# A mixture of experts computed only for the chosen tokens, with rows sorted by expert through DRAM, in place of every expert for every token

## The reference

```python
def _moe_forward(hidden_states, gate_w, gate_bias, eg_w, eu_w, ed_w, sg_w, su_w, sd_w):
    x = hidden_states.reshape(-1, H)
    shared = jax.nn.silu(x @ sg_w.T) * (x @ su_w.T) @ sd_w.T
    scores = jax.nn.sigmoid(x @ gate_w.T) + gate_bias
    group_scores = scores.reshape(T, G, E // G).max(axis=-1)
    _, sel_groups = lax.top_k(group_scores, TG)
    ...
    topk_w, topk_i = lax.top_k(masked_scores, K)
    topk_w = topk_w / (topk_w.sum(axis=-1, keepdims=True) + 1e-08)
    comb = jnp.zeros((T, E), x.dtype).at[jnp.arange(T)[:, None], topk_i].add(topk_w)
    h = silu(einsum('th,eih->eti', x, eg_w)) * einsum('th,eih->eti', x, eu_w)
    routed = jnp.einsum('eti,ehi,te->th', h, ed_w, comb)
    return (shared + routed).reshape(B, S, H)
```

## Time and profile before

| | us |
| --- | --- |
| median of three runs (1149.51, 1150.63, 1157.2) | 1150.63 |
| span of the profiled execution | 1143.3 |
| start and full attention (0 to 421.5) | 421.5 |
| experts M1 (421.5 to 713) | 291.5 |
| banded attention (713 to 861) | 148.0 |
| experts M2 (861 to 1143.3) | 282.3 |
| PE busy, share of the span | 1044.1, 91% |
| DVE busy, share of the span | 925.3, 81% |

### The profile page before, as it was taken

How to read it: one execution, slowest core, us unless ns; L and a number is a source line. 1 busy time by engine, 2 the same in 40 slices (tenths; PEclk the granted TensorE clock), 3 DMA queues, 4 the chain that set the end, 5 groups by cost and what they waited for, 6 DMA issues and landing times. The chain is left out here.

```text
span 1143.3 us, 18866 instructions
## 1 busy us (share of the span) xinstructions
PE 1044.1 (91%) x6314; PEld 427.5 (37%) x6314; DVE 925.3 (81%) x2139; ACT 709.0 (62%) x1089; POOL 461.7 (40%) x434
## 2 busy tenths in 40 slices
PE   5769999999999979999999998888888999999998
PEld 4212222222222325444444443334444444444443
DVE  8688999999998467889788776877876779877775
ACT  2537778777787765666666664355465566666664
POOL 4116336532100105565564554100113556556554
PEclk9758999999999989999999999679999999999999
DMA  6901302311200126566764873142206667687662
GB/s 207 253 2 28 81 9 72 80 53 28 54 2 1 43 59 170 163 170 174 196 181 140 218 193 81 34 110 59 72 4 172 157 152 188 171 208 193 182 189 57
DMA packets 72185, 131.63 MB, mean 115 GB/s; under 512 B 12680, under 2 KB 47624, under 8 KB 72088
## 3 DMA queue, kind: packets, MB, share of 16 engines
q1 hardware_dynamic: 68704, 120.92, 40.5%
q10 hardware_dynamic: 3384, 9.51, 3.1%
HBM read 115.08 MB, written 14.91 MB: 114 GB/s over the span
## 5 line engine op out<-in xcount | busy, mean ns | idle before, releaser
L421 ACT ACTIVATE Aatt_prob<-Aatt_st 128x1024 f32<-128x1024 f32 x256 | 247.7, 1022 | 66.1 <-PE Aatt_st L315 65.1
L487 DVE TENSOR_REDUCE Aatt_mx<-Aatt_sc 128x1 f32<-128x512 f32 x439 | 273.3, 683 | 10.0 <-PE Aatt_sc L302 9.5
L1993 POOL TENSOR_TENSOR M1ex_low<-M1ex_hid,M1ex_high 128x512 f16<-128x512 f32 x132 | 152.8, 1157 | 136.2 <-ACT M1ex_high L1892 70.1
L1993 POOL TENSOR_TENSOR M2ex_low<-M2ex_hid,M2ex_high 128x512 f16<-128x512 f32 x132 | 152.7, 1157 | 130.8 <-PE M2ex_acc L1848 73.3
L302 PE MATMUL Aatt_sc<-ks,qs 48*128 48x512 bf16 x496 | 152.5, 408 | 29.5 <-DVE Aatt_mx L487 11.8
L1886 ACT ACTIVATE M2ex_sil<-M2ex_ring,unscale 128x512 f32<-128x512 f32 x132 | 90.7, 687 | 95.3 <-PE M2ex_ring L1831 95.1
L1886 ACT ACTIVATE M1ex_sil<-M1ex_ring,unscale 128x512 f32<-128x512 f32 x132 | 90.7, 687 | 89.4 <-PE M1ex_ring L1831 88.9
L327 PE MATMUL Aatt_pv<-Aatt_prob,vg 128*32 128x512 f32 x1024 | 137.9, 611 | 0.6 <-ACT Aatt_prob L421 0.6
L1930 DVE SCALAR_TENSOR_TENSOR M2ex_ring<-M2ex_ring,unscale,M2ex_sil 128x512 f32<-128x512 f32 x132 | 100.0, 757 | 42.0 <-ACT M2ex_sil L1886 38.9
L1930 DVE SCALAR_TENSOR_TENSOR M1ex_ring<-M1ex_ring,unscale,M1ex_sil 128x512 f32<-128x512 f32 x132 | 99.9, 757 | 36.2 <-ACT M1ex_sil L1886 32.9
L302 PEld LDWEIGHTS Aatt_sc<-ks,qs 48*128 48x128 bf16 x496 | 35.9, 94 | 201.1 <-DVE Aatt_mx L487 167.7
(11 more groups left out here) (437 smaller groups left out, 1959.5 us busy)
## 6 DMA issues: line engine op xcount, KB each, us to landing
M1ex_cb<-comb SPq DMA_DIRECT2D x130, 256.0 KB, 4.1
M2ex_cb<-comb SPq DMA_DIRECT2D x130, 256.0 KB, 4.2
M_wt<-wsplit SPq DMA_DIRECT2D x132, 192.0 KB, 4.0
wsplit<-split_cut SPq DMA_DIRECT2D x9, 704.0 KB, 4.5
qs<-stack SPq DMA_DIRECT2D x32, 96.0 KB
ks<-stack SPq DMA_DIRECT2D x30, 96.0 KB
split_raw<-in_wg_dram ACTq DMA_DIRECT2D x3, 704.0 KB, 8.5
split_raw<-in_wu_dram ACTq DMA_DIRECT2D x3, 704.0 KB, 12.0
```

What stands on the lines that cost most here:

```text
L421: act.activation(prob[e % 4][:, :, :].rearrange("p a c -> p (a c)"), st[pr][:, :, :].rearrange("p a c -> p (a c)"), ACT.Exp, scale=SCALE). ...
L487: ins = dve.tensor_reduce(mx[k][:, m, h:h + 1], scores, AX.X, ALU.max)
L1993: pool.tensor_tensor(low[q % 3][:, :], hid[q % 3][:, :], high[q % 3][:, :], ALU.subtract).then_inc(low_ready, 1)
```

## The change

In both layers of experts, each token's normalised row (high and low f16 part beside each other, 512 bytes) is now sent to the experts that it chose, and only those are computed.

- **Dispatch.** After the routing, new code (`dispatch_tensor`, `dispatch_vector`) counts the tokens of each expert, gives each expert as many blocks of 128 rows as it needs, and works out for each of a token's six choices the row in which it stands (`index`), and for each block the offset of its expert's weights (`expert`). A batch has a fixed number of 112 blocks, enough for any routing; blocks that are not needed are computed too.
- **Scatter.** POOL issues 48 indirect DMAs per batch (8 tiles of 128 tokens times 6 choices); each writes 128 rows to `slots_in` in DRAM.
- **Blocks.** Four blocks make a quad, 28 quads per batch, N = 56. SP loads a quad (512 rows, 256 KB) with a DMA that transposes it into one of three buffers, PE multiplies with the rows as the stationary side and with weights at an offset read from a register, and SP stores the quad's result rows (256 KB) to `slots_out`. Of a quad, `gate_up` has 12 matmuls of 128 columns and waits for its load and for `gate_times_up` of the quad two before; `turn` has four transposes, `down` eight matmuls. DVE copies the result out of PSUM (`evict`, 128x512) before it is stored. All routed weights lie in SBUF.
- **Gather.** POOL issues 48 indirect DMAs per batch that fetch each token's six result rows, and DVE adds them up with their weights (`combine`).
- **Order.** The output projection, normalisation, routing and dispatch of batch 1 and the shared expert now stand ahead of the loop over quads, and the normalisation and projection of batch 0 behind it.
- **Zero fill.** Since some rows of `slots_in` are never written, ACT issues two DMAs at the start of `attend_full` that fill both (14336 rows of 512 bytes each) with zeros.
- **Stores of split weights.** The nine pieces go to three tables instead of `wsplit`: six pieces in runs of 256 bytes, three in four DMAs each with runs of 512 bytes.
- **Removed.** `comb`, its turning, copies, store and loads; the weight loads per pair; POOL's low parts of the experts.

```diff
@@ attend_full
         def _(act):
             act.sem_inc(exp_done, FREE)
+            for rows in env.slots_in:
+                act.dma_start(rows.rearrange("(p a) c -> p a c", p=P),
+                              env.zero[:, :].rearrange("p (a c) -> p a c", a=1).to_broadcast([P, BLOCKS, 2 * C])).then_inc(env.zeroed, 16)
...
-            rest_of(route_vector(dve, env, q1))
-            for c in range(2):
-                dve.wait_ge(q1.comb_turned, c + 1)
-                dve.tensor_copy(q1.combT[:, c * CH:(c + 1) * CH], bank[c][0:ROWS, :]).then_inc(q1.comb_copied, 1)
+            rest_of(route_vector(dve, env, n1, q1, send))
+            rest_of(dispatch_vector(dve, env, q1, send, bank))
...
+def dispatch_vector(dve, env, q, send, bank):
...
+    dve.wait_ge(send.counted, 1)
+    done(dve.tensor_scalar(send.count[:, :], bank[1][:, 0:E], float(P - 1), None, ALU.add))
...
+    done(dve.tensor_tensor_scan(send.ends[:, :], env.ones_row[:, :], send.blocks[:, :], 0.0, ALU.mult, ALU.add))
...
+    dve.scalar_tensor_tensor(send.place[:, :, :], bank[0][:, :].rearrange("p (t e) -> p t e", t=TB), 1.0,
+                             q.of_experts.keep[:, :, :], ALU.add, ALU.mult).then_inc(send.place_ready, 1)
...
+    for t in range(TB):
+        dve.max(send.top[:, t, :], send.place[:, t, :]).then_inc(send.step, 1)
...
+    dve.tensor_scalar(send.index[:, :, :], send.top[:, :, :], 1.0, None, ALU.subtract).then_inc(send.index_ready, 1)
...
+def scatter_rows(pool, env, send, b):
...
+    pool.wait_ge(env.zeroed, 16 * B)
+    if b:
+        pool.wait_ge(send.index_ready, 1)
+        pool.wait_ge(send.low_ready, 2)
+    for t in range(TB):
+        for k in range(SLOTS):
+            pool.indirect_dma_start(env.slots_in[b], bass.IndirectOffsetOnAxis(
+                ap=send.index[:, t, k:k + 1].bitcast(U32), axis=0), send.row[:, t, :], None).then_inc(env.scattered[b], 16)
+            yield
...
@@ experts, SP
+            def load_quad(i):
+                b, g = i // QUADS, i % QUADS
+                if g == 0:
+                    sp.wait_ge(env.scattered[b], ALL_SENT)
+                if i >= X_RING:
+                    sp.wait_ge(gu_done, i - X_RING + 1)
+                sp.dma_start_transpose(rows_in[i % X_RING][:, :, :],
+                                       env.slots_in[b][g * CH:(g + 1) * CH, :]).then_inc(rows_loaded[i % X_RING], 16)
...
+            for i in range(N + 5):
+                if i < N:
+                    load_quad(i)
+                if i >= 5:
+                    store_quad(i - 5)
@@ experts, PE
+            rest_of(out_tensor(pe, env, o, bank, 1))
+            rest_of(norm_of_batch_tensor(pe, env, n1, bank))
+            rest_of(route_tensor(pe, env, n1, q1, bank))
+            rest_of(dispatch_tensor(pe, env, q1, sends[1], bank))
...
+            for i in range(N + 3):
+                if i < N:
+                    gate_up(i)
+                if 2 <= i < N + 2:
+                    turn(i - 2)
+                if i >= 3:
+                    down(i - 3)
@@ experts, DVE
+            for i in range(N + 4):
+                if i < N:
+                    gate_times_up(i)
+                if 1 <= i < N + 1:
+                    low_part(i - 1)
+                if i >= 4:
+                    evict(i - 4)
...
+                if i >= QUADS + 9 and (i - QUADS) % 3 == 0 and (i - QUADS - 9) // 3 < TB:
+                    combine((i - QUADS - 9) // 3)
@@ experts, POOL
+            rows = scatter_rows(pool, env, sends[0], 0)
+            for _ in range(16):
+                next(rows)
+            rest_of(norm_of_batch_gpsimd(pool, env, n1))
+            for _ in range(12):
+                next(rows)
+            rest_of(route_gpsimd(pool, env, n1, q1, sends[1], 1))
+            rest_of(rows)
+            rest_of(scatter_rows(pool, env, sends[1], 1))
+            for j in range(2 * TB):
+                gather(j)
```

More of the change, by code:

```diff
@@ L1564, in route_vector @@
     of_groups, of_experts = q.of_groups, q.of_experts
-    yield
-    yield
+    for c in range(2):
+        tiles = slice(4 * c, 4 * c + 4)
+        dve.wait_ge(n.xn_ready, 4 * c + 4)
+        dve.tensor_copy(send.row[:, tiles, 0:C], n.xn[:, tiles, :]).then_inc(send.high_ready, 1)
+        yield
     yield
@@ L1817, in _, with weights_of @@
         def _(pe):
[L1818 to L1821 removed]
+            registers = [[pe.alloc_register(f"{tag}_expert{i}_{j}") for j in range(4 * GROUP)] for i in range(2)]
+            of_block = {}
+            def weights_of(i):
+                b, g = i // QUADS, i % QUADS
+                handles = registers[i // GROUP % 2]
+                pe.load(handles, sends[b].expert[0:1, 4 * g:4 * g + 4 * GROUP])
+                for j, h in enumerate(handles):
+                    of_block[4 * i + j] = pe.snap(h, min_val=0, max_val=(E - 1) * 2 * P)
@@ new lines, in gate_up @@
+            def gate_up(i):
+                b, g = i // QUADS, i % QUADS
+                if i == QUADS:
+                    pe.wait_ge(sends[1].expert_ready, 1)
+                if g % GROUP == 0:
+                    weights_of(i)
+                pe.wait_ge(rows_loaded[i % X_RING], 16 * (i // X_RING + 1))
+                if i >= 2:
+                    pe.wait_ge(hid_ready, i - 1)
+                x = rows_in[i % X_RING]
+                for j in range(4):
+                    w = first[:, bass.ds(of_block[4 * i + j], 2 * P)].rearrange("p (g h c) -> p h g c", g=2, h=2)
+                    to = gu[i % 2][:, j * P:(j + 1) * P].rearrange("p (g c) -> p g c", g=2)
+                    rows = slice(j * P, (j + 1) * P)
+                    pe.matmul(to, x[:, 0, rows], w[:, 0, :, :], start=True, stop=False)
+                    pe.matmul(to, x[:, 0, rows], w[:, 1, :, :], start=False, stop=False)
+                    mm = pe.matmul(to, x[:, 1, rows], w[:, 0, :, :], start=False, stop=True)
+                mm.then_inc(gu_done, 1)
@@ L1866, in _ @@
-            beside, behind = before(), after()
-            for q in range(QN):
-                gate_up(q)
-                if q < HB:
-                    next(beside, None)
-                if q in (UPDATE, UPDATE + 1):
-                    back(0, q - UPDATE)
-                if q >= AFTER:
-                    next(behind, None)
-                if q >= LAG:
-                    down(q - LAG)
-            for q in range(QN - LAG, QN):
-                down(q)
-            for c in range(2):
-                back(1, c)
+                if c:
+                    pe.wait_ge(s_hid, c)
@@ L1900, in before @@
-            def before():
-                yield from out_scalar(act, env, o, bank, 1)
-                yield from norm_of_batch_scalar(act, env, n1, bank)
-                yield from route_scalar(act, env, n1, q1, bank, 1)
-            def after():
-                if not last:
-                    yield from norm_of_batch_scalar(act, env, n2, bank)
-                    yield from qkv_scalar(act, env, v2, bank, 0)
-            beside, behind = before(), after()
-            for q in range(QN):
-                silu(q)
-                if q:
-                    high_part(q - 1)
-                if q in (HB + LAG - 1, HB + LAG):
-                    add_up(0, q - HB - LAG + 1)
-                if q < HB:
-                    next(beside, None)
-                if q >= AFTER:
-                    next(behind, None)
@@ new lines, in _ @@
+            rest_of(out_scalar(act, env, o, bank, 1))
+            rest_of(norm_of_batch_scalar(act, env, n1, bank))
+            rest_of(route_scalar(act, env, n1, q1, bank, 1))
+            for c in range(NC):
+                shared(c)
+            for i in range(N + 2):
+                if i < N:
+                    silu(i)
+                if 1 <= i < N + 1:
+                    high_part(i - 1)
+                if i >= 2:
+                    copy_turned(i - 2)
+            if not last:
+                rest_of(norm_of_batch_scalar(act, env, n2, bank))
+                rest_of(qkv_scalar(act, env, v2, bank, 0))
@@ L1955, in after @@
-            def after():
-                if not last:
-                    dve.wait_ge(x_ready, 2)
-                    yield from norm_of_batch_vector(dve, env, n2, 0)
-                    yield from qkv_vector(dve, env, v2, bank, 0)
-            dve.tensor_copy(cb[0][:, :], env.unscale[:, 3:4].to_broadcast([P, S])).then_inc(cb_filled, 1)
-            dve.wait_ge(cb_filled, 1)
-            beside, behind = before(), after()
-            for q in range(QN):
-                times_up(q)
-                times_weight(q)
-                if q < HB:
-                    next(beside, None)
-                if q in (UPDATE, UPDATE + 1):
-                    update(0, q - UPDATE)
-                if q >= AFTER:
-                    next(behind, None)
@@ new lines, in _ @@
+            after = iter(())
+            if not last:
+                dve.wait_ge(combined, TB)
+                after = norm_of_batch_vector(dve, env, n2, 0)
+                for _ in range(6):
```

(8 more changed lines are left out.)

591 lines of the change are left out of this document (361 added, 230 removed).

## The result

The changed kernel takes 1367.47 us (median of four runs, 1354.11 to 1374.09) against 1150.07: a ratio of 1.188, 95% interval 1.180 to 1.196. It is slower by 217 us; 1487 was forecast. Its profiled execution has a span of 1367.0 us, 223.7 more than the span before.

| stage | before | after | difference | forecast |
| --- | --- | --- | --- | --- |
| start and full attention, to 421.87 / 459.40 | 421.9 | 459.4 | +37.5 | +59 |
| experts M1 | 288.7 | 375.6 | +87.0 | +133 |
| banded attention | 150.5 | 162.4 | +11.9 | +4 |
| experts M2, to the end | 282.3 | 369.6 | +87.3 | +140 |

A forecast was written before the change was run, and what follows sets the result against it. PE's matmuls bound M1 and M2; a ring of waits through SP's order would replace them. Span 1143.3 + 55 (zero fill) + 8 (dispatch) + 133 (M1) + 140 (M2) = 1479.3, plus 7.3: 1487 us; 8-in-10 range 1310 to 1710.

The forecast's parts named there:

- The loop: 56 quads in each of M1 and M2: 4.9 us per quad (3.8 to 6.4), 274 us per stage.
- The ring: Loop over quads: each load stands behind an earlier quad's store in SP's order; two quads take 9.8 us.
- L: Landing time of a quad's transposing load in the loop: 4.6 us, bounds 2.4 and 7.6.
- The four handovers: Waits between engines within two quads of the loop: 1.1 us together, an estimate.
- Ahead of the loop: Start of each experts stage: PE ready after 70.5 us, POOL's path ends at 73; loop starts at 74.
- c: What one indirect DMA costs POOL in scatters and gathers: 1.2 us, from 0.21 or 0.37 up to 2.86.
- Behind the loop: After the last quad: 8 us to finish and store, then gathers; 62 and 4 more in M2, 65 in M1.
- The zero fill: Start of full attention: two DMAs hold ACT's queue for 58 us, +55 (bounds 0 and 60).
- Dispatch: In both attentions it takes the place of turning and storing `comb`: +4 us each, +8.
- POOL as the pace: Rival, chance 0.15: indirect DMAs cost POOL 2 us or 2.86 us each; total about 1610 or 1810 us.
- The dearer load: Rival, chance 0.15: transposing load goes in eight pieces, landing 3.6 us later, 6.7 us per quad, total 1690.
- The fast rival: Rival, chance 0.10: engines pace the loop, 56 quads in 148 us, zero fill holds nobody; 1112 us, 3% faster.

The follow-up runs named there:

- the later store: Changed kernel with SP storing each quad's result one step later, behind i - 6 instead of i - 5: 1276.16 us, 1.112 of the kernel before.
- 72 blocks: 72 blocks per batch in place of 112, against the kernel with result stores one step later, zero fill on SP and scatters first: 1151.12 us, 0.999 of before.
- cutting its waits there: Against the 72-block kernel of 1151.12 us: POOL's five products for batch 1 made by DVE, six empty steps between batches on every engine: 1127.77 us, 0.982 of before.
- the opened ring: Changed kernel with result stores one step later: 1276.16 us with the transposing load, 1257.78 us with a plain load in its place.

## Why the prediction was right, and where it was off

**What bounds the kernel** was read rightly: the matmuls went (PE 1044 to 866 us busy) and the time rose, since what took their place is latency.

**The loop** was the largest error: 274 us forecast, 213.5 and 212.0 measured. That alone is 122 us too much, where the whole sum (1479.3 for the span) lay 112 too high; the other errors, on both sides, about cancel. The ring was the right mechanism, as the later store shows. Its terms were mis-sized: two quads take 7.6 us, not 9.8. The landing L was 3.6 to 3.7 at the median, not 4.6, some 1 us of the 2.2: I took it from plain loads of the same size, but a plain load in this very place lands after 3.3. L lay inside its bounds of 2.4 to 7.6. The four handovers, 1.1 us without a row, take some 0.3 together in the chain, 0.8 less, and the store's issue 0.36, not 0.5. Each is small, but the ring turns 56 times in the two loops.

The 0.11 us of a matmul of 128 columns was a wrong reading of the earlier trace rows: those four are of f32, at the upper clock. By the row of 512 columns in f16, 0.22, it is 0.055. That `gate_up` still took 1.3 to 1.5 us in the turns of the chain, near the 1.6 forecast, is luck: the clock was at its lower level for much of the loop.

The Trainium skill, "VectorE: DVE Perf Modes", section "The three transpose paths", gives 1309 ns for a 128x128 transpose by DMA, by which I estimated 10.5 us for a quad's eight. The trace does not agree with that use of it: 3.6 to 3.7 us at the median, so the eight do not follow each other.

**Ahead of the loop**, 74 was right within 2 us, for partly another reason. I let POOL wait for `inv` of batch 1 at 41 us; in the trace it never waited, because 28 scatters and four products kept it busy until 43 us. What decides is simply 48 x 1.26 and 7 us of products. c = 1.2 was near, 1.26, but by luck: its row is of an elementwise operation, and an indirect DMA's price stood in no row.

**Behind the loop** I put 8 for the drain and the last store; it was 13.6. Of the six stores that follow the last load, the last one was issued 10.5 us behind the last `gate_up`, since its quad still had to be turned, go down and be evicted. The gathers were 48 x 1.26 + 3, as forecast. In M1 I had the gathers wait for the projection (the ring of three buffers); they did not: POOL issued them from 762 to 825 without such a wait, and the 86 us are drain, gathers and the barrier.

**The zero fill** held ACT, +37.5 and not +55: the step that failed is that the issues last as long as both transfers. They lasted 39.1 us, about as long as the first transfer (41.9), while the second DMA landed 73.4 us after its issue. The Trainium skill, "Perfetto Trace Analysis", section "DMA Instruction — HWDGE (DVE, Sync)", lets the sequencer go on when all descriptors are generated; the trace agrees, with ACT free at 73 and the data there at 108.

**Dispatch** cost nothing in the full attention where +4 was forecast. In the banded attention the stage is 11.9 us longer. Its granted clock by stretch, the changed kernel and then the kernel before (columns as in the earlier trace rows), at the same distance from the stage's start:

```profile
923.00:931.00 8.00, 8.00 (x51) 4.42 (x50) 4.53 (x24) 1.90 (x6) 0.00 (x0) 0.50 0.00 0
963.00:971.00 8.00, 8.00 (x56) 5.15 (x52) 4.25 (x24) 3.56 (x10) 0.00 (x0) 0.50 0.00 1
```

```profile
798.50:806.50 8.00, 7.04 (x83) 4.61 (x83) 6.68 (x38) 3.59 (x10) 0.91 (x4) 1.00 0.01 3
838.50:846.50 8.00, 6.72 (x93) 2.71 (x88) 7.66 (x40) 4.70 (x13) 3.26 (x6) 1.00 0.03 6
```

The clock fell to its lower level (1.2 GHz) in two stretches where the kernel before had the upper one (2.4 GHz). Of the eleven traces of the changed kernel and its variants, all with the same code in this stage, eight have 161 to 163 us here and three 153 to 156, and the one of these that I read by stretch (154.0, with the later store) keeps the upper level from 80 us into the stage on. So some 8 of the 11.9 us come with the lower clock, in the same code. The 3 to 4 that are left look like the 4 forecast for dispatch, but they aren't: from the end of the last `keep` of the routing to the first PE instruction of M2, where dispatch stands in place of `comb`, it is 8.2 us in the kernel before, 9.5 in the changed kernel and 8.0 with the later store. They are lost ahead of that, and where, like what lowered the clock, stays open.

**The rivals.** POOL as the pace did not decide here, but it comes close with 72 blocks: 192 x 1.26 = 242 of the 280 us of a stage, and cutting its waits there brought 23 us. The dearer load fell. The fast rival needed 2.4 us per quad to draw level; the ring gave 3.8, and the opened loop 3.0.

## What to carry to other kernels

Before sparse work replaces dense work, count the ring of waits that one unit of it goes through in each engine's order, queues included: here 261 us of matmuls per stage gave way to 212 us of a ring, 75 ahead of it and 83 behind it. A store and the next load in one in-order queue tie the load to the store's producer; one more step of delay between them was worth 89 us in the two loops. An indirect DMA cost nearly the same time for 64 rows as for 128, so indirect DMAs have to be counted as instructions, and units kept for the worst case cost as much as used ones: 40 of 112 blocks per batch were worth 95 us.

## What the runs showed of the hardware that was not expected

- An indirect DMA took POOL 0.96 us for 128 rows of 512 bytes and 0.89 us for 64, with 0.30 us between two of them.
- A transposing load of 256 KB landed 0.3 to 0.4 us behind a plain one (3.6 to 3.7 against 3.3 us at the median). Its issue held SP for 1.27 us against 0.51, and with the opened ring, at the same 205 GB/s, it kept the DMA engines busy for 0.97 of the time, the plain one for 0.73.
- Of two DMAs of 7.3 MB in runs of 512 bytes, one behind the other in ACT's queue, the first held the queue for 0.63 us and the second for 38.44, to 2.8 us before the first landed; the second landed 73.4 us after its issue.
